# Moving a convolution's matmuls into the threshold stage of a two-layer kernel, with a one-pass count check and relocated buffer fills

## What is computed

```python
x = x + tanh(g_xattn[0]) * attention(layernorm(x), ctx, ctx)
# L0 ffn: z = x_n @ ternary(W_syn).T + b_syn            (1024 wide)
#         thresh = the 102nd largest of each row of z
#         hidden = where(z >= thresh, relu(z), 0)
#         layernorm(x_n + hidden @ ternary(W_out).T + b_out)
x = x + tanh(g_ffn[0]) * L0_ffn(layernorm(x))
# L1 xattn, 16 heads of 8 channels, along L=256 positions:
kv  = einsum('bhil,bhjl->bijhl', k_, v_)                # k_ = v_ = ctx
y   = irfft(rfft(kv, 2L) * rfft(ssm_kernel, 2L))[..., :L]
out = einsum('bijhl,bhil->bjhl', y + kv * D, q_)        # q_ = layernorm(x)
x = x + tanh(g_xattn[1]) * out
# L1 ffn: softmax router over 64 experts, top 6, plus a shared expert
x = x + tanh(g_ffn[1]) * moe(layernorm(x))
```

## Time and profile before

| what | us |
|---|---|
| median of 3 runs | 857.5 (854.87 to 858.48) |
| the profiled execution, its own time | 852.39 |
| its span | 850.7 |
| mean granted clock of TensorE | 0.897 of full speed |
| busy: PE / DVE / POOL / ACT | 629.0 / 529.8 / 466.0 / 276.4 |
| first blocks / threshold / projection | 146 / 83.5 / 93.5 |
| convolution and routing / gap / experts and end | 185 / 12 / 330.7 |

### The profile page before, as it was taken

One profiled execution on the slowest core, in us unless ns is written; L12 is line 12 of the kernel. 1 busy time (PEld: TensorE's weight loads), 2 busy tenths in 40 slices (PEclk: granted clock), 3 DMA queues, 4 the chain that ended last, 5 costly groups with the idle time before them and its releaser, 6 DMA issues.

```text
span 850.7 us, 12240 instructions
## 1 busy us (share of the span) xinstructions
PE 629.0 (74%) x2970; PEld 477.1 (56%) x2970; DVE 529.8 (62%) x1693; ACT 276.4 (32%) x599; POOL 466.0 (55%) x503
## 2 busy tenths in 40 slices
PE   1378997000199877799988648999999999999940
PEld 1234553000187764566766436888888888888720
DVE  3778875999868776898978324553443443544422
ACT  1113334769523320233434312232232332332200
POOL 5448786465022220177756660567677677676662
PEclk9779999555599998999999878999999999999985
DMA  7325566787000206445542525899999999999587
GB/s 269 143 99 173 180 213 238 295 337 290 1 12 26 91 25 200 155 172 175 192 167 85 189 105 192 203 252 254 226 254 248 229 264 234 244 252 242 76 184 231
DMA packets 84835, 157.80 MB, mean 185 GB/s; under 512 B 10688, under 2 KB 55168, under 8 KB 84800
## 3 DMA queue, kind: packets, MB, share of 16 engines
q1 hardware_dynamic: 54144, 103.23, 36.7%
q0 software_dynamic: 29792, 53.25, 26.6%
q10 hardware_dynamic: 864, 0.93, 0.3%
HBM read 88.66 MB, written 68.70 MB: 185 GB/s over the span
## 4 chain that ended last, share of the span: by engine, by line
PE 60%; DVE 15%; issue 8%; DMA 5%; ACT 5%; POOL 2%; another core or an unknown queue 1%; DVEq 1%; SPq 1%; ACTq 1%; POOLq 0%
PE psum L967 13%; PE psum L757 7%; PE psum L971 6%; PE psum L980 6%; PE psum L985 4%; PE psum L955 4%; PE psum L797 3%; PE psum L898 2%; PE psum L887 2%; DMA acc<-hh,toki 2%; DVE qT L1378 2%; PE psum L829 2%; PE psum L830 2%; PE psum L831 2%; PE psum L739 2%
## 5 line engine op out<-in xcount | busy, mean ns | idle before, releaser
L690 POOL DMA_INDIRECT acc<-hh,toki x128 | 199.1, 1555 | 98.4 <-DVE hh L1748 56.5
L1748 DVE TENSOR_SCALAR hh<-psum,wtok 128x256 f32<-128x256 f32 x128 | 56.0, 479 | 155.1 <-DMA acc<-hh,toki 103.7
L653 POOL DMA_INDIRECT xs_rows<-Z,slot x96 | 98.4, 1025 | 44.2 <-issue 28.0
L967 PE MATMUL psum<-qT,Z 128*128 128x256 f32 x512 | 121.3, 380 | 0.4 <-ACT qT L1184 0.4
L967 PEld LDWEIGHTS psum<-qT,Z 128*128 128x128 f32 x512 | 92.3, 190 | 10.9 <-issue 0.9
L579 POOL TENSOR_TENSOR rstd<-mv,neghalf 128x1 f32<-128x1 f32 (+1 forms) x48 | 30.7, 639 | 109.2 <-DVE mv L1250 109.2
L757 PE MATMUL psum<-wt,hTs 128*128 128x512 f32 x128 | 61.8, 628 | 12.6 <-ACT hTs L1061 7.7
L1184 ACT ACTIVATE qT<-psum 128x512 f32<-128x512 f32 x64 | 38.1, 597 | 95.1 <-PE psum L955 93.2
L971 PE MATMUL psum<-qT,Z 128*112 128x256 f32 x256 | 65.7, 379 | 0.0
L980 PE MATMUL psum<-Z,hh 128*128 128x256 f32 x256 | 60.6, 379 | 1.2 <-DVE hh L1738 1.2
L780 PE MATMUL psum<-bad,onesf 128*128 128x1 f32 x2 | 0.6, 348 | 79.4 <-DVE bad L1438 79.4
(11 more groups left out here) (288 smaller groups left out, 1333.4 us busy)
## 6 DMA issues: line engine op xcount, KB each, us to landing
Z<-in_wexp SPq DMA_DIRECT2D x66, 496.0 KB
xs_rows<-fill POOLq DMA_DIRECT2D x64, 272.0 KB, 2.8
Z<-xs_rows SPq DMA_DIRECT2D x64, 272.0 KB
Z<-kv_rows SPq DMA_DIRECT2D x16, 688.0 KB
kv_rows<-Z SPq DMA_DIRECT2D x12, 688.0 KB, 3.9
acc<-fill POOLq DMA_DIRECT2D x4, 1024.0 KB, 8.3
ctxH_s<-in_ctxH SPq DMA_DIRECT2D x16, 224.0 KB, 3.9
wt<-in_wd SPq DMA_DIRECT2D x66, 48.0 KB
```

Source lines behind the costliest of these rows:

```text
L653: pool.indirect_dma_start(out=xs_rows[:, :], out_offset=bass.IndirectOffsetOnAxis(ap=slot[:, t, k:k + 1], axis=0), in_=H[:, t, :], in_offs ...
L690: pool.indirect_dma_start(out=acc[s % 2][:, :], out_offset=bass.IndirectOffsetOnAxis(ap=toki[:, g, j:j + 1], axis=0), in_=y_sb[:, s, j, :] ...
L967: m = pe.matmul(pA[par][:, g * CAP:(g + 1) * CAP], wgu_sb[:, s, k, g * P:(g + 1) * P], xT[:, par, k, :], start=(k == 0), stop=(k == 1))
L1748: m = dve.tensor_scalar(y_sb[:, s, j, :], pY[par][:, j * D:(j + 1) * D], wtok[:, g, j:j + 1], None, ALU.mult)
```

## The change

What it does:

- `conv` runs for all 16 heads on PE after the last `z` tile, ahead of the matmul on `bad`. It reads `kv` from a new buffer `kvb` and writes PSUM halves by the head's parity. ACT copies each head's result to SBUF (`keep_conv`): two heads after each of the rounds 1 to 3, one after check tiles 1, 4, 7, 10 and 13, five after the last. SP stores them to a new HBM tensor `co_rows` (688 KB per head) and in the routing stage loads them back where it loaded `kv_rows` and the filter. `tdiag` is formed by POOL.
- PE waits for the last `keep_conv` before the matmul on `bad`.
- The check is one pass (Sign with the sum), the counts are read before the last two tiles' maxima and `bad` is made after them with two more small operations.
- The fills of `acc` go from POOL to SP, between the last `ctx` loads and the last three heads' stores. The fills of `xs_rows` go from POOL in the threshold stage to SP in the projection stage, four after each tile's row store.
- In the routing stage PE keeps only turns, router, ranks and the shared expert, with PSUM banks of their own and fewer waits, in a new order; `times_q` reads the loaded result from SBUF.

The diff, cut:

```diff
@@ SP @@
+            sp.wait_ge(p_step, 2)
+            for a_ in acc:
+                for c in range(T // P // 8):
+                    sp.dma_start(a_[8 * c * P:8 * (c + 1) * P, :].rearrange("(p r) d -> p r d", r=8),
+                                   fill[:, 0:1, 0:D].to_broadcast([P, 8, D])).then_inc(filled, 16)
...
             keep_kv(NH - 3)
             load_ctxH(NH - 1)
...
+            for h in range(NH):
+                if h + 2 < NH:
+                    sp.wait_ge(conv_done, h + 1)
+                    load_toep(h + 2, h % 2)
+                    load_kv(h + 2, h % 2)
+                sp.wait_ge(co_ready, h + 1)
+                sp.dma_start(co_rows[h], co[h % 2]).then_inc(co_out[h % 2], 16)
...
             for b in range(NT):
                 sp.wait_ge(var4_ready, b + 1)
...
+                for e in range(b * E // NT, (b + 1) * E // NT):
+                    sp.dma_start(rows_v[e, 0:CAP, :].rearrange("(p b) d -> p (b d)", b=2),
+                                 fill[:, :, :].rearrange("p b d -> p (b d)")).then_inc(filled, 16)
...
             for h in range(2, NH):
-                sp.wait_ge(conv_done, h - 1)
-                load_toep(h, h % 2)
-                load_kv(h, h % 2)
+                sp.wait_ge(prod_done, h - 1)
+                load_co(h, h % 2)
@@ POOL @@
+            for h in range(NH):
+                par = h % 2
+                if h >= 2:
+                    pool.wait_ge(conv_done, h - 1)
+                pool.tensor_scalar(tdiag[:, par, :], ident[:, :], D_b[:, h:h + 1], None, ALU.mult).then_inc(tdiag_ready, 1)
+                pool.wait_ge(head_in[par], 16 * (h // 2) + 16)
+                pool.wait_ge(tdiag_ready, 2 * h + 1)
+                pool.tensor_tensor(tdiag[:, par, :], tdiag[:, par, :], toep_s[:, par, 0, :], ALU.add).then_inc(tdiag_ready, 1)
@@ PE @@
+            def conv(h):
+                par = h % 2
+                pe.wait_ge(kv_in[par], 16 * (h // 2) + 16)
+                pe.wait_ge(tdiag_ready, 2 * h + 2)
+                if h >= 2:
+                    pe.wait_ge(co_ready, h - 1)
...
+            pe.wait_ge(z_ready, NT)
+            for h in range(1, NH):
+                conv(h)
+            pe.wait_ge(co_ready, NH)
             pe.wait_ge(w_ready, 2)
             pe.wait_ge(bad_ready, 1)
...
@@ ACT @@
+            def keep_conv(h):
+                par = h % 2
+                act.wait_ge(conv_done, h + 1)
+                if h >= 2:
+                    act.wait_ge(co_out[par], 16 * (h // 2))
+                for l in range(2):
+                    m = act.activation(co[par][:, l * NT * NCOL:(l + 1) * NT * NCOL].rearrange("p (g n) -> p g n", g=2),
+                                       psum[:, 4 * par + 2 * l:4 * par + 2 * l + 2, 0:8 * NCOL], ACT.Copy)
+                m.then_inc(co_ready, 1)
...
+            for t in range(NT):
+                verify(t)
+                if t % 3 == 1:
+                    keep_conv(h)
+                    h += 1
+            while h < NH:
+                keep_conv(h)
+                h += 1
@@ DVE @@
             def times_q(h):
-                dve.wait_ge(conv_done, h + 1)
+                dve.wait_ge(kv_in[h % 2], 16 * (NH // 2 + h // 2) + 16)
...
-                Y = psum[:, at_:at_ + 4, 0:8 * NCOL].rearrange("p g (b r) -> p g b r", r=NCOL)
+                Y = kv[:, h % 2].rearrange("p m (g b) r -> p (m g) b r", b=8)
```

More of the change, by code:

```diff
@@ L432, in load_kv, with load_co @@
             def load_kv(h, par):
-                sp.dma_start(kv[:, par].rearrange("p m b r -> p (m b r)"), kv_rows[h]).then_inc(kv_in[par], 16)
-            load_toep(0, 0)
-            load_toep(1, 1)
+                if h < EARLY_HEADS:
+                    sp.wait_ge(kv_out[h % 3], 16 * (h // 3) + 16)
+                else:
+                    sp.wait_ge(kvq_out[h % 2], 16 * ((h - EARLY_HEADS) // 2) + 16)
+                sp.dma_start(kvb[:, par].rearrange("p m b r -> p (m b r)"), kv_rows[h]).then_inc(kv_in[par], 16)
+            def load_co(h, par):
+                sp.wait_ge(co_out[par], 16 * (h // 2) + 16)
+                sp.dma_start(kv[:, par].rearrange("p m b r -> p (m b r)"), co_rows[h]).then_inc(kv_in[par], 16)
+            for h in range(2):
+                load_toep(h, h)
+                load_kv(h, h)
             sp.dma_start(gate_sb[:, :, :], gateT).then_inc(gate_in, 16)
@@ L903, in _ @@
             pe.wait_ge(hidT_ready, NT)
-            conv(0)
             pe.wait_ge(qT_ready, NT)
@@ L1091, in _, with verify @@
                 act.wait_ge(cnt_done, NT + (NT - NTD) * r)
+                keep_conv(2 * r - 2)
+                keep_conv(2 * r - 1)
             act.wait_ge(thr_ready, ROUNDS + 1)
-            for half in range(2):
-                first, end = half * NTD, half * NTD + NTD
-                if half:
-                    act.wait_ge(below_done, first)
-                with act.Fori(first, end) as t:
-                    act.activation(junk[:, t - first, :], z[:, t, :], ACT.Relu, bias=hib[:, bass.ds(t, 1)],
-                                   scale=-BIG).then_inc(above_done, 1)
-                act.wait_ge(above_done, end)
-                with act.Fori(first, end) as t:
-                    act.activation(junk[:, t - first, :], junk[:, t - first, :], ACT.Sign,
-                                   accum_out=below[:, bass.ds(t, 1)]).then_inc(below_done, 1)
+            def verify(t):
+                if t >= NTD:
+                    act.wait_ge(below_done, t - NTD + 1)
+                act.activation(junk[:, t % NTD, :], z[:, t, :], ACT.Sign, bias=hib[:, t:t + 1], scale=-BIG,
+                               accum_out=below[:, t:t + 1]).then_inc(below_done, 1)
+            h = 2 * ROUNDS - 2
+            for t in range(NT):
[6 more added lines that the diff above has]
+                h += 1
             def evac_hidden(b, par):
@@ L1444, in _ @@
                 if t == NT - 2:
-                    verdict()
+                    counts()
                 dve.wait_ge(masked, t + 1)
```

166 lines of the change are left out of this document (66 added, 100 removed).

## The result

The changed kernel takes 868.4 us (867.2 to 873.6, 4 runs) against 856.7 us (854.9 to 858.5, 4 runs) of the kernel before: a ratio of 1.016, 95% interval 1.012 to 1.020. I had forecast 854.5 us and a range up to 866. The profiled execution has a span of 865.1 us against 850.7, 14.4 us more.

The account below looks back on a forecast made before the run. DVE's chain was taken to bound the threshold stage and PE to be busiest in routing. +7.5 (threshold) and -10.4 (routing and start of experts) made -2.9 on the profiled 852.4, 849.5; plus 5.1 to the median, 854.5 us, range 846 to 866.

Parts of the forecast that it names:

- term 2: Threshold stage: the last heads' convolutions end late and delay the read of `bad` to 235.1 against 227.58, +7.5 us.
- term 1: End of the first blocks: `acc` fills on SP delay the `ctxH` load; last `z` +2 us (0 to +3), within term 2.
- term 4: Routing stage: the wait for conv(0) goes and pair periods shorten, -8 us at the last slot (-13 to -3).
- term 5: Start of the experts: a shared product now comes before the ranks, -2.4 us; the 10.63 us idle time stays.
- The slack I had counted: Before the turn of the last tile's result: some 4.2 us that could absorb the late last products on POOL.
- Term 3: Projection stage: 64 fills (17.8 MB) moved to SP are hidden by DVE, cost 0 (0 to +1 us).
- The -4.4 at the seam: Start of the routing stage: the 5.44 us wait for conv(0) goes, about 1 us for `q`'s last turn remains.
- The -3.5 in the periods: Seven pair periods of routing: shorter without convolution, partly offset by PE's lower clock; -3.5 us, bounds -9 and +1.
- the stall goes: Before the experts: the 10.63 us idle time disappears, +7.5 - 16.2 = -8.7 us, giving 849; chance 0.20.
- the convolution chain is bound by PE at 1.2 GHz or by late loads: Threshold stage, heads 6 to 15: five heads at low clock add 13.5 us (868), all give 881; chance 0.15.
- shut out by `times_q`: Routing stage: nine SBUF operations per head hold POOL's scatters 2.3 us on average, +23 us, giving 877; chance 0.08.

Follow-up runs that it names:

- e2: The changed kernel with SP's six fills of `acc` queued behind the loads of the shared weights: 866.6 us, ratio 1.014.
- e3: The changed kernel without the loads of `kv` for heads 2 to 15 in the threshold stage (wrong output): 861.3 us in a single run.
- e4: The changed kernel with seven idle 128x344 matmuls per pair behind the shared expert's first product, in TensorE's gap: 874.8 us, ratio 1.021.
- e5: The kernel of e2 with five idle 128x512 matmuls per pair, at the place where e4 had its seven: 869.3 us, ratio 1.018.

## Why the prediction was wrong

A small gain was forecast and a loss came out, above all by two terms of the sum. Against the profiled execution the sum had -2.9 us and the span came out +14.4. Of the 17.3 between them 11.6 lie in term 2 (with term 1 in it: 19.1 against 7.5), 6.7 in term 4 (-1.3 against -8) and 0.6 in term 5; the experts' stage took 1.6 off.

- **Term 1, the fills, was right in kind and too small.** I put the load of `ctxH` at 136 to 139 and took +2, of 0 to +3, for the last `z`. The products started at 139.50, just past the end of what I had allowed, and `z` came 5.4 us later. I had SP issue a fill in 0.43 us; it took 1.8 on the mean, and the load had to wait for all six (issued at 132.25). The slack I had counted, 4.2 us, was nearly there: of 7.4 us only 3.65 reached the turn of the last tile. What I had left out is that TensorE waits in that time (3.71 us) and runs the last `z` at a clock of 0.73, which made it 1.7 us longer. e2 gives the 5 us back.
- **Term 2, "the trace shows 3.9 us for a 688 KB transfer; with a load and a store per head on the queue 4.9 is possible, and I take 4.4", is the step that failed.** With a load and a store per head on the queue it took up to 7.2 us from issue to conv. I had the pace per head at 4.2 us; from conv(9) to conv(15) it was 5.2. From the end of the rounds to the read of `bad` it took 53.3 us where the sum had 45.3. The 3.9 was the median of twelve stores in the first blocks, where the DMA share was 0.46 (20 to 120 us), and no load. e3 puts the price of the loads at 11 us. That DVE's chain would be over before the convolution was right; low clock had a small part in the delay (1.8 us in conv(14)). The sum's own steps give 235.4 for the read of `bad`, not 235.1.
- **Term 3, nothing in the projection stage, was right**: from the read of `bad` to the first `times_q` less its wait, both kernels take the same 96 us, with 17.8 MB of fills in it.
- **Term 4, -8, was -1.3** (15.1 - 19.1 at the start, +2.6 over seven periods). The -4.4 at the seam was right to 0.4 us. The -3.5 in the periods was +2.6, outside the bounds of -9 and +1 that I gave. The working said that TensorE would idle some 7 us a pair and lose clock, and priced that at 1 us a pair; e4 and e5 show about 2, because turn, logits and the second shared product all lie on the way from DVE's moments to the ranks. The periods without an unexplained idle time were 17.6 to 18.2 us before; after they are 19.6 on the mean.
- **Term 5, -2.4 behind the last slots, was -1.8 at the first use of expert rows, by another way.** At the mark of the term, TensorE's first turn of expert rows, it was -8.0 (530.31 after the last slot result at 509.86; 520.55 after 492.07), but DVE used the first rows only at 540.97, and there most of it was gone. The sums of the overflow did come 2.5 us sooner behind the slots, and the idle time of 10.63 us that I had left as it is did go (2.33). But now the scatters bound: the last one began 15.1 us after the last slot result (14.4 before), and the second clearing scatter waited 6.55 us for the first, beside the loads of rows and weights, where it had waited 3.54. My rival "the stall goes" had priced it at 5.8 us more; it gave nothing, since the next bound stood closer than I had put it.
- **The rivals.** The slow one, "the convolution chain is bound by PE at 1.2 GHz or by late loads", came true by its second half, and `bad` moved by 19.1 us, past the 14.7 that I had named as the point of decision; it got a chance of 0.15. The scatters were not shut out by `times_q`: 96 of them took 98.3 us against 98.4, and where one began with the nine operations it took 1.26 instead of 0.96 in most pairs, 1.46 in the first.

The Trainium skill ("SBUF — State Buffer", "SBUF: two separate sides") has the lock held for the whole of one instruction. I read this so that POOL gets in between two, and the trace agrees with that reading: beside the nine operations the longest scatter took 1.46 us, 0.5 more than alone, and not the 2.3 more of the rival.

## What to carry to other kernels

When work is moved into a stage where its engine is idle, price what it brings with it: here 1.5 MB of DMA per head, whose landing is read from rows with as many transfers on the queue and in the same direction, not from a quiet stretch. And ask what the engine it leaves will do in the gap: TensorE's clock fell where the convolution had filled it, and the short chains of matmuls that others wait for became slower. The gain sat at the seam into the routing stage; moving two heads of sixteen, and a third to the end of the stage before, took it, and moving all sixteen cost more than it brought.

## What was not expected of the hardware

- A 688 KB load took 4.7 us from issue to use where no store had been issued for 7.7 us (head 9), and 6.9 to 7.2 us for heads 12 to 14, with stores of the same size between the loads (DMA share 0.84). Heads 10 and 11 took 5.0 with such stores too, so the stores alone don't explain the step. A store took 3.3 us without the loads (e3) and 5.5 to 7.2 with them.
- ACT can stand idle for up to 9 us just behind a table load, every second pair of the routing stage, in some kernels (e4, e5), while others with the same instructions on ACT (after, e2) show it only behind these pairs (5.27 us before 521.73; 8.21 before 523.56), but for 2.51 us in e2, and no semaphore or DMA that the profile knows ends it. The runs of one kernel scatter by 14 us (845.8 to 859.8 in 23 runs of the kernel before), which these idle times may explain; no run here shows that they do.
